# A transformer block on one core: the down projection in fp32r hi/lo parts instead of fp32

## The reference

```python
x = x + attn(xn, Wq, Wkv, Wout, bout) + ffn(xn, w_gate, w_up, w_down)

def fp4_quant_dequant(x):          # blocks of 16 along the last axis
    scale = maximum(max(abs(xb)) / 6.0, 1e-12)
    q = _GRID[searchsorted(_MID, abs(xb / scale))] * sign(xb) * scale

def fp4_linear(x, w):              # (..., k) by (n, k)
    return einsum('bsk,nk->bsn', fp4_quant_dequant(x), fp4_quant_dequant(w))

gate = fp4_linear(x, w_gate)       # 256 -> 704
y = fp4_linear(x, w_up)            # 256 -> 704
h = silu(gate) * y
return fp4_linear(h, w_down)       # 704 -> 256
```

## Time and profile before

| | us |
|---|---|
| median of 3 runs | 2087.13 (2086.47 to 2089.76) |
| profiled execution, its own time | 2086.47 |
| its span in the profile | 2084.4 |
| PE busy | 1888.5 (91%) |
| DVE busy | 1556.3 (75%) |
| ACT busy | 826.0 (40%) |
| POOL busy | 1516.5 (73%) |

### The profile page before, as it was taken

How to read it: one execution, slowest core, us unless ns; L and a number is a source line. 1 busy time by engine, 2 the same in 40 slices (tenths; PEclk the granted TensorE clock), 3 DMA queues, 4 the chain that set the end, 5 groups by cost and what they waited for, 6 DMA issues and landing times. The chain is left out here.

```text
span 2084.4 us, 30067 instructions
## 1 busy us (share of the span) xinstructions
PE 1888.5 (91%) x11300; PEld 1198.1 (57%) x11300; DVE 1556.3 (75%) x1967; ACT 826.0 (40%) x1068; POOL 1516.5 (73%) x699
## 2 busy tenths in 40 slices
PE   1288989669999999999999999999999999999499
PEld 0277888435555555555555555555555555555299
DVE  8699999467777777777777777777777777775154
ACT  1222332114444444444444444444444444444232
POOL 2356555218888888888888888888888888888444
PEclk9999999869999999999999999999999999999799
DMA  8100101300111121111112111111211111101286
GB/s 295 50 31 33 56 33 58 114 21 26 46 33 42 50 69 37 52 32 47 42 37 82 32 47 32 54 34 47 80 39 42 32 47 32 32 27 32 95 291 212
DMA packets 132282, 129.80 MB, mean 62 GB/s; under 512 B 40880, under 2 KB 96816, under 8 KB 132016
## 3 DMA queue, kind: packets, MB, share of 16 engines
q1 hardware_dynamic: 132144, 127.96, 19.4%
HBM read 87.56 MB, written 40.37 MB: 61 GB/s over the span
## 5 line engine op out<-in xcount | busy, mean ns | idle before, releaser
L1046 POOL TENSOR_TENSOR acc<-acc,prob 128x1024 f32<-128x1024 f32 x384 | 939.0, 2445 | 154.2 <-ACT prob L1089 125.8
L927 DVE TENSOR_REDUCE half_max<-m_ps 128x2 f32<-128x1024 f32 x512 | 625.4, 1221 | 340.2 <-PE m_ps L800 337.7
L1089 ACT ACTIVATE prob<-s_ps 128x1024 f32<-128x1024 f32 x512 | 498.4, 1025 | 362.0 <-PE s_ps L824 278.2
L839 PE MATMUL o_ps<-prob,v 128*64 128x512 f32 x2048 | 492.5, 602 | 0.0
L839 PEld LDWEIGHTS o_ps<-prob,v 128*64 128x64 f32 x2048 | 130.0, 136 | 250.8 <-issue 183.7
L1028 POOL TENSOR_TENSOR turned<-straight,shuffled 128x512 f32<-128x512 f32 x128 | 191.5, 1496 | 82.5 <-DVE shuffled L959 82.5
L800 PE MATMUL m_ps<-k_hi,q_hi 64*128 64x512 f32 x1024 | 233.3, 451 | 16.7 <-DVE half_max L927 14.4
L869 PE MATMUL misc_ps<-xT,wqk 128*128 128x512 f32 x768 | 219.2, 422 | 18.3 <-DMA xT<-xn_scratch 10.8
L869 PEld LDWEIGHTS misc_ps<-xT,wqk 128*128 128x128 f32 x768 | 138.9, 194 | 143.6 <-issue 109.0
L821 PE MATMUL s_ps<-q_hi,k_hi 64*128 64x512 f32 x1024 | 203.8, 393 | 0.0
L821 PE MATMUL s_ps<-q_lo,k_hi 64*128 64x512 f32 x1024 | 202.4, 390 | 0.0
(11 more groups left out here) (126 smaller groups left out, 2419.7 us busy)
## 6 DMA issues: line engine op xcount, KB each, us to landing
wqk<-wp_scratch SPq DMA_DIRECT2D x32, 512.0 KB, 4.1
inv_rows<-inv_scratch SPq DMA_DIRECT2D x128, 128.0 KB, 2.9
o_scratch<-o_norm SPq DMA_DIRECT2D x64, 256.0 KB, 2.0
o_in<-o_scratch SPq DMA_DIRECT2D x8, 2048.0 KB, 10.8
xn_scratch<-xnT SPq DMA_DIRECT2D x8, 1024.0 KB, 4.3
xT<-xn_scratch SPq DMA_DIRECT2D x8, 1024.0 KB, 5.8
wv<-wp_scratch SPq DMA_DIRECT2D x32, 256.0 KB, 3.5
wp_scratch<-wp_hl SPq DMA_DIRECT2D x8, 768.0 KB, 4.0
```

The lines of the kernel that those rows point to most:

```text
L839: ins = nc.tensor.matmul(o_ps[head * DH:(head + 1) * DH, :], v[s // 2 % 2][:, kt, s % 2, at:at + DH], prob[n % SLOTS][:, head, :], start=k ...
L927: nc.vector.tensor_reduce(half_max[:, half % 2, :, t % GRP, part], m_ps[:, :, :], axis=AX.X, op=ALU.max, negate=True).then_inc(half_maxed, 1)
L1046: nc.gpsimd.tensor_tensor(acc[b][:, :, :], first, prob[n % SLOTS][:, :, :], ALU.add).then_inc(added, 1)
L1089: nc.scalar.activation(prob[n % SLOTS][:, :, :], s_ps[n % 2][:, :, :], ACT.Exp).then_inc(exp_done, 1)
```

## The change

`hT` and `wdT` become fp32r tiles with a HI and a LO part. `high_h` writes the HI part as before; a new `low_h(n)` on VectorE writes the LO part of hT, 128 x 768, from PSUM, and `down` waits for it. `down` has 18 matmuls where it had 6, one for each of the three products and each chunk. `low_h(n - 2)` stands in VectorE's step n between the scales and the rounding; two more stand behind the last group. In `weights_part` two `low_parts` (1024 and 512 columns) are added behind the last instruction of VectorE.

```diff
--- before.py
+++ after.py
@@ -173,7 +173,7 @@
             yield src[:, 0:FF], [wgT[:, h, c, w, :] for h in (HI, LO)]
         else:
             k = min(4, FT - c)
-            yield src[:, 0:k * D], [wdT[:, c * D:(c + k) * D]]
+            yield src[:, 0:k * D], [wdT[:, h, c * D:(c + k) * D] for h in (HI, LO)]
 
     with nc.Block() as block:
         @block.sync
@@ -277,6 +277,8 @@
             chain.link(v.scalar_tensor_tensor(out=rstd[:, :], in0=total, scalar=1.5, in1=root, op0=ALU.add, op1=ALU.mult))
             dve.wait_ge(chain_s, chain.n)
             v.scalar_tensor_tensor(out=kept["shift"][:, :], in0=mean[:, :], scalar=-1.0, in1=rstd[:, :], op0=ALU.mult, op1=ALU.mult)
+            for n in range(4, len(units)):
+                low_parts(n)
 
         @block.scalar
         def _(act):
@@ -347,7 +349,7 @@
     sg = sb("sg", [P, FF], F32)
     h = sb("h", [P, FF], F32)
     hq = sb("hq", [P, FPAD], F32)
-    hT = sb("hT", [P, FT, P], F32)
+    hT = sb("hT", [P, 2, FT, P], F32R)
     res = sb("res", [P, 2, D], F32)
     turn = psum("turn", [P, 2 * 512], F32)
     x_ps = psum("x_ps", [P, 512], F32)
@@ -362,7 +364,7 @@
     x_turned, x_high, x_low = sem("x_turned"), sem("x_high"), sem("x_low")
     xn_stored = sem("xn_stored")
     gate_up, silu_done, h_done, hq_ready = sem("gate_up"), sem("silu_done"), sem("h_done"), sem("hq_ready")
-    h_turned, h_high, down_done = sem("h_turned"), sem("h_high"), sem("down_done")
+    h_turned, h_high, h_low, down_done = sem("h_turned"), sem("h_high"), sem("h_low"), sem("down_done")
     res_ready, res_stored = sem("res_ready"), [sem(f"res_stored{i}") for i in range(2)]
     x_all, mean, rstd, ident = kept["x_all"], kept["mean"], kept["rstd"], kept["ident"]
     wgT, wdT = kept["wgT"], kept["wdT"]
@@ -423,6 +425,12 @@
                 ins = nc.vector.tensor_tensor(to[:, LO], src, to[:, HI].bitcast(F32), ALU.subtract)
                 if i == 1:
                     ins.then_inc(x_low, 1)
+
+            def low_h(n):
+
+                dve.wait_ge(h_high, n + 1)
+                nc.vector.tensor_tensor(hT[:, LO, :, :], turn[:, 0:FPAD].rearrange("p (c n) -> p c n", c=FT),
+                                        hT[:, HI, :, :].bitcast(F32), ALU.subtract).then_inc(h_low, 1)
 
             def group(g, u):
                 chain.turn(first_ops + g * GRP * H_OPS)
@@ -440,6 +448,8 @@
                                             up_ps[:, :, 0:FH], ALU.mult).then_inc(h_done, 1)
                     dve.wait_ge(h_done, n + 1)
                     block_scales(nc, chain, h[:, :], h_tmp(t), later)
+                    if not early:
+                        low_h(n - 2)
                     if not (type(n) is int and n == 0):
 
                         dve.wait_ge(hq_ready, n)
@@ -466,6 +476,8 @@
                 for i in range(2):
                     low_x(t, t, i)
             groups(dve, group)
+            for t in (GRP - 2, GRP - 1):
+                low_h(TILES - GRP + t)
 
         @block.gpsimd
         def _(pool):
@@ -543,7 +555,7 @@
                 if not (type(n) is int and n == 0):
 
                     act.wait_ge(down_done, n)
-                nc.scalar.activation(hT[:, :, :], turn[:, 0:FPAD].rearrange("p (c n) -> p c n", c=FT),
+                nc.scalar.activation(hT[:, HI, :, :], turn[:, 0:FPAD].rearrange("p (c n) -> p c n", c=FT),
                                      ACT.Copy).then_inc(h_high, 1)
 
             def silu(n):
@@ -615,12 +627,16 @@
                 ins.then_inc(h_turned, 1)
 
             def down(n):
-                pe.wait_ge(h_high, n + 1)
+                pe.wait_ge(h_low, n + 1)
                 if not (type(n) is int and n == 0):
 
                     pe.wait_ge(res_ready, n)
-                for j in range(FT):
-                    ins = nc.tensor.matmul(down_ps[:, 0:D], hT[:, j, :], wdT[:, j * D:(j + 1) * D], start=j == 0, stop=j == FT - 1)
+                k = 0
+                for hs, ws in PARTS:
+                    for j in range(FT):
+                        ins = nc.tensor.matmul(down_ps[:, 0:D], hT[:, hs, j, :], wdT[:, ws, j * D:(j + 1) * D],
+                                               start=k == 0, stop=k == 3 * FT - 1)
+                        k += 1
                 ins.then_inc(down_done, 1)
 
             def group(g, u):
@@ -1369,7 +1385,7 @@
             hold("rstd", [P, TILES], F32)
             hold("shift", [P, TILES], F32)
             hold("wgT", [P, 2, DC, 2, FF], F32R)
-            hold("wdT", [P, FT * D], F32)
+            hold("wdT", [P, 2, FT * D], F32R)
             part(weights_part)
             part(ffn_part)
         part(attention_part)
```

## The result

The changed kernel takes 2121.1 us (median of 4 runs, 2120.07 to 2123.33) against 2086.8 us, a ratio of 1.0168 (95% interval 1.0152 to 1.0183): 34.3 us slower. I had forecast slower, with 2108.5 us and 2103 to 2116 as the range; the time lies outside it. 21.7 us of the 34.3 had a term in my sum.

The account below looks back on a forecast made before the run. VectorE was taken as the bound in groups 0 to 5. The terms 1.8 + 14.1 + 3.5 + 1.2 + 0.8 + 0.3 = 21.7 us, on 2086.47, led to a forecast of 2108.5 us, range 2103 to 2116.

Parts of the forecast that it names:

- VectorE is the bound; the saving on TensorE is worth nothing.: Groups 0 to 5: VectorE, 96% busy, sets the pace, so the 0.39 us saved per down counts as nothing.
- L432 costs 0.88 us, at t = 2 nothing.: Groups 0 to 5: 16 tiles pay 0.88 us each, 14.1 us; at t = 2 L116 waits for GpSimd anyway.
- that rival: At t = 2, GpSimd holds L432 up: 1.3 us in six groups, 7.8 us, so 2116; 6 in 100.
- Tiles 24 to 27: VectorE has no idle time in these four steps, so 4 x 0.88 = 3.5 us.
- Tiles 28 to 30: Three steps follow VectorE at 7.2 us each, 21.7 against 20.5: +1.2 us, ends -1 and +3.
- Weights part: Two low parts behind VectorE's last instruction, with no other engine on the path: +1.8 us, ends 1.7 and 1.9.
- The wait of x_amax for xn, +0.3 in all.: At t = 3 xn comes 0.8 to 0.9 us later, VectorE 0.88 later: +0.06 us each at most.
- my rival: TensorE's clock falls behind the new gap at t = 3, down and turn 1.7 us longer: 8.5 us, 2117; 9 in 100.
- Both covers hold: Steady steps: turn and gate queued behind down's wait delay neither silu (4 to 5 us slack) nor GpSimd's hq.
- the tail at +0.8: Last h to last down: L432 of tile 31 +1.0, a shorter down -0.4, some wait for tile 30's L432.
- The attention as long as before.: The attention, behind the feed-forward part, was to keep its length; a change there would prove the forecast wrong.
- The range: Whole kernel: 2103 to 2116 us, taking in part of the clock's case; the forecast's own ends were 2105 and 2113.

Follow-up runs that it names:

- e3_no_low: Changed kernel without any L432; the 6 LO-part matmuls of down read hT's HI part, and down waits only for high_h's HI part: 2093.1 us, 1.0033.
- the kept-busy run: Changed kernel with added useless matmuls on TensorE before down's wait for L432 (12 per tile, 6 for tiles 24 to 28, 34 for tile 29): 2114.3 us, 1.012.
- the second pair of profiles: Changed kernel and kernel before each profiled once more, no edit: 2119.5 us and 2086.2 us.

## Why the prediction was wrong, step by step

- **VectorE is the bound; the saving on TensorE is worth nothing.** Right. A down is 2.22 us from start to start of what follows (2.21 forecast), and nothing came of it; without L432 and its wait (e3_no_low) the steps are 1.5 us shorter in all.
- **L432 costs 0.88 us, at t = 2 nothing.** Right, and measured by the steps: t = 1 to 2 is 9.56 us (9.56 forecast), t = 2 11.91, t = 3 9.59. GpSimd doesn't hold it: it takes 0.96 us inside L119, and that rival is out. L116 starts 0.87 us behind it (287.48 to 288.35).
- **Tiles 24 to 27** +3.5: right. **Tiles 28 to 30** +1.2, measured +2.1, inside its bounds: in two of the three steps L96 takes 1.39 us and ends when GpSimd's hq ends, and each is 7.7 us where I had 7.2.
- **Weights part** +1.8: right. The table has +2.0, of which 0.2 is that the part ran later in this execution; counted from L121 it is 1.77.
- **The wait of x_amax for xn, +0.3 in all.** Wrong: +4.8. I worked it out with TensorE at 2.4 GHz in the new down. The gaps came nearly as my rival had them (1.67 and 2.27 us at t = 2, 2.65 at t = 3, for 2.3, 2.3 and 2.8). In three of five groups the down of t = 3 ran at 1.2 GHz, 1.4 us longer, and the wait was 2.1 us; in the two others the fall came at the up ahead of it, and the wait was 0.7, as my working has it. With TensorE kept busy all five are 0.7 to 0.8. The mechanism stood among the rivals, at 9 in 100 and 8.5 us; it came true in part.
- **"Both covers hold"** and the tail at +0.8. Wrong, and the largest miss: +6.5. I had checked the wait of `down` in the steady steps only, where a late down has 4 to 5 us of slack, and in the tail I counted the L432 of tile 31 in full, that of tile 30 at 0.2 us and that of tile 29 at nothing, all at the full clock. In the tail there is no slack: each of the last three downs is on the path, and each waits for its own L432. By the rows:

```profile
404.09 0.96 DVE L432 TENSOR_TENSOR hT<-turn,hT 128x768 fp32r<-128x768 f32 x1
...
411.24 0.96 DVE L432 TENSOR_TENSOR hT<-turn,hT 128x768 fp32r<-128x768 f32 x1 [3.34 <-ACT hT L558]
417.69 0.96 DVE L432 TENSOR_TENSOR hT<-turn,hT 128x768 fp32r<-128x768 f32 x1 [5.50 <-ACT hT L558]
```

```profile
405.10 4.21 PE L637 MATMUL down_ps<-wdT,hT 128*128 128x256 f32 x18 [4.57 <-DVE hT L432]
409.11 1.25 PE L626 MATMUL turn<-ident,hq 128*128 128x128 f32 x6
412.25 3.28 PE L637 MATMUL down_ps<-wdT,hT 128*128 128x256 f32 x18 [1.89 <-DVE hT L432]
415.33 1.48 PE L626 MATMUL turn<-ident,hq 128*128 128x128 f32 x6
418.71 3.01 PE L637 MATMUL down_ps<-wdT,hT 128*128 128x256 f32 x18 [1.89 <-DVE hT L432]
```

  and the same place in the kernel before:

```profile
378.29 2.86 PE L623 MATMUL down_ps<-wdT,hT 128*128 128x256 f32 x12 [0.90 <-ACT hT L546]
380.98 0.82 PE L614 MATMUL turn<-ident,hq 128*128 128x128 f32 x6
382.70 2.86 PE L623 MATMUL down_ps<-wdT,hT 128*128 128x256 f32 x12 [0.90 <-ACT hT L546]
385.39 0.82 PE L614 MATMUL turn<-ident,hq 128*128 128x128 f32 x6
```

  The down of tile 29 starts 4.9 us behind the last h, since its L432 stands behind the scales of tile 31; it started 3.3 behind it (+1.6). Each of the two later downs waits for one more L432 between turn and down, 1.0 us each by the kept-busy run (2.71 us from 403.49 to 406.20, where it was 1.72). That is +3.6 of waiting, and three shorter downs take 1.4 off: 2.2, what the kept-busy run left standing. The other 4.3 us are the clock: behind 4.57 us of idle time the first down takes 4.01 us to its turn (2.22 when kept busy), the next 3.08 to its turn and the last 3.01 to its end (2.24 and 2.38), and the turns 1.25 and 1.48 instead of 0.82.
- **The attention as long as before.** Not quite: +2.0 at its start (+1.4 in the second pair of profiles). 1.3 of it is the third chunk at 1.2 GHz; the rest is open.
- **The range.** It had no case for the tail. With the tail (+5.7) and x_amax (+4.5) put right the sum is 31.9 us; measured are 34.3. Of the 12.6 us that I missed, 8.1 are TensorE's clock in the feed-forward part, a case that I had priced in one of its two places, 2.2 the waits of the tail less its shorter downs (where I had 0.8), and 1.3 the clock at the start of the attention.

## What to carry to other kernels

A new wait has to be priced twice: in the steady loop, where a slack can cover it, and in the drain at the end, where the same instructions form a chain and each wait counts once per remaining tile. Where an engine's time is spent held up by another, the place of an added instruction decides its price: with the same 22 instructions groups 0 to 5 are 18.9 us longer when they stand behind the held ones (about 14 us of it are their own time, the rest the wait of x_amax) and 2.1 longer in front of them. And a wait need stand only ahead of the products that use the late operand; that order was worth 12 us here.

## What the runs showed of the hardware

TensorE's clock fell for longer although its longest wait had become shorter. In groups 1 to 5 of the changed kernel no wait of TensorE is over 2.7 us (before there was one of 4.07 in each), but there are more of them: in groups 0 to 5 it stands idle 52 us in all, where it was 33. It is at 1.2 GHz for longer: a mean granted clock of 0.92 in groups 0 to 5 is about 6.5 us at half speed in each, 0.95 before is 3.7 (one less the mean, over 0.5, of a sixth of the stretch). In the group whose rows are shown above the clock fell at 301 us, behind waits of 1.67, 2.27 and 2.65 us with 5.0 and 2.6 us of matmuls between them. And a kernel whose matmuls are cheaper can lose the saving to this: with no L432 at all the last down took 4.21 us instead of 2.38. Keeping TensorE busy with matmuls that do nothing made the changed kernel 6.8 us faster.
